# Features of q and k laid head-inside in each block of 128, and the transfers into the stack merged to one per slot and group of four heads

## The chip, the cores and the metric

One core of one Trainium2 chip. The metric is the device time of one execution in microseconds (us); the whole program is one launch.

## The reference, cut to what matters

Two cross-attention layers run one after the other over a batch of 16, with 256 query rows, width D = 512, 16 heads of 32 features. Layer 0 has a fused key/value projection over the 512 rows of context and query together, biases, an RMS norm and an MLP of hidden width 2048; layer 1 has a layer norm on the context, 256 keys and a gate. All in float32.

```
# layer 0 (b, 256 queries, 512 keys)
q  = (latents @ q_w + q_b).reshape(b, k_len, 16, 32)
kv = (concat(x, latents) @ kv_w + kv_b).reshape(b, p + k_len, 16, 32, 2)
attn = softmax(where(mask, einsum('bkhd,bnhd->bhkn', q, k) / 32, -inf))
a = einsum('bhkn,bnhd->bkhd', attn, v).reshape(b, k_len, 512) @ out_w + out_b + latents
out = gelu(rmsnorm(a) @ mlp_w1 + mlp_b1) @ mlp_w2 + mlp_b2 + latents
# layer 1 (b, 256 queries, 256 keys)
a = layer_norm(audio_kv);  Q = h @ Wq.T;  K = a @ Wk.T;  V = a @ Wv.T
attn = softmax(where(mask, Q K^T * 32**-0.5, -inf))
out = h + tanh(gate) * ((attn V) @ Wo.T)
```

Which of the 512 features of q and k sits in which row of an intermediate tile is free, as long as q and k agree and each head meets its own 32 features.

## The kernel before

The program is three stages: attention layer 0 (`attention_layer` with layer = 0), the MLP (`mlp`), attention layer 1. Both attention layers run the same code, one batch element per iteration, software-pipelined: iteration (p, a) prepares the projections of element p while the attention of element a = p - 1 runs. There are 15 iterations of a layer in which both halves are at work; the instruction streams of TensorE, VectorE, ScalarE, GpSimd and SyncE are written out by hand, each in its own block, tied by semaphores.

Numbers keep three products of float32 split in a high and a low part. For q and k this goes through the stack: a tile `stack` of 99 rows by 16 heads by 768 (layer 0) or 512 (layer 1) columns. Rows 0 to 31 (slot 0) hold a head's 32 high features of q and k, slot 1 (rows 32 to 63) q high beside k low, slot 2 (rows 64 to 95) q low beside k high; row 96 is the mask, rows 97 and 98 the softmax shift in two parts. One matmul with 97 rows then gives a head's scores (line 934), and one with 99 rows gives them shifted and transposed (line 959). The projections leave q and k in `qk` (layer 0: in `room`) with 128 feature rows to a block, that is four heads of 32 rows under each other, for four blocks g = 0 to 3. A half is two blocks, or eight heads.

SyncE (SP) issues every transfer, in order. In `load_stacks` (lines 307 to 321) it issues for each half and each j = 0 to 3 four transfers (32 rows, the two heads 4g + j of the half): 16 of them on line 311, and one for the mask row on line 319. SP's iteration (lines 363 to 405) is, in order: residual rows (367), layer 0's normalised rows out (370), next tokens (304, 305), then for each half the wait for `shift_copied` (ScalarE's line 538), two transfers of 8 rows of `shiftT` into rows 97 and 98 of the stack (379) and `spread_inverse` (354 to 361): eight transfers, each one row of reciprocals of the row sums spread over 32 rows of `norm_room` (359). Then `load_stacks` of both halves behind the wait on line 401 (TensorE has issued the last line 959 matmuls that read that half), and layer 1's output (405).

TensorE waits for a half of the stack at its first score (line 931), for the shift rows of a half at line 952, VectorE for the reciprocals of a half at line 712 before `normalise` (713), and TensorE's `project` (979) of block g needs that block normalised. ScalarE may write `qk` of the next element once the stack has been loaded from it (lines 512 and 517). In layer 0 the normalised values feed `turn_shift` and v through `o_norm_done` as well.

Weights are split into a high part (ScalarE, line 488) and a low part (VectorE, line 626) once per layer; the per-feature vectors are loaded on line 339 with a count `VECTORS` that GpSimd waits for before its memset of the stack (lines 465 and 470).

## Time and profile before

| | us |
|---|---|
| median of three executions (2630.4 to 2631.77) | 2631.36 |
| the profiled execution, its own time | 2632.31 |
| its span, first to last instruction | 2630.5 |
| TensorE matmul busy (share of the span) | 2443.7 (93%) |
| ScalarE busy | 1472.5 (56%) |
| VectorE busy | 1170.5 (44%) |

The stages by the clock of the trace: layer 0 to about 1100 us, the MLP to about 1823 us, layer 1 from there to the end. A row of the profile gives the engine (PE is TensorE's matmul, PEld its weight load, DVE VectorE, ACT ScalarE, POOL GpSimd, SPq SyncE's issue of transfers), and l_ before a name stands for either layer's tile. Lines 64 to 66 are the helper `product`, used by all projections and the MLP.

### The profile page before, as it was taken

The numbers are of one execution on the slowest core, as the hardware profiler recorded it, in microseconds if no ns is written. First come the engines' busy times: TensorE is split into PE (matmuls) and PEld (weight loads), VectorE is DVE, ScalarE is ACT, GpSimd is POOL, SyncE is SP. The second block draws the span as 40 slices with busy tenths as digits, with TensorE's granted clock in tenths as the row PEclk, the third lists the DMA queues.
The fourth block names the chain that finished last, engine by engine and source line by source line (L and its number), as shares of the span: only waits on it lengthen the run. The fifth ranks groups of instructions, "written<-read, shape, count | busy, mean of one in ns | idle before, by whom it ended". The sixth has DMA issues, their size and how long they took to land. (4 is left out here: it accounts for less than half of the span.)

```text
span 2630.5 us, 43959 instructions
## 1 busy us (share of the span) xinstructions
PE 2443.7 (93%) x14528; PEld 1913.9 (73%) x14528; DVE 1170.5 (44%) x2222; ACT 1472.5 (56%) x3354; POOL 226.2 (9%) x252
## 2 busy tenths in 40 slices
PE   6999999999999999899999999998888888888887
PEld 5677777777777777478888888887767677676674
DVE  4455555555555555452212221122655455455553
ACT  3777777777777777552222222222556566566564
POOL 1000000000000000000000000001211112112110
PEclk8999999999999999799999999999999999999998
DMA  6555555555555555341101110121566665656655
GB/s 173 106 114 113 113 113 113 113 113 113 109 115 112 112 112 97 76 140 49 48 0 48 48 48 0 48 80 64 106 130 124 118 138 102 127 131 109 132 100 86
DMA packets 172764, 255.82 MB, mean 97 GB/s; under 512 B 33793, under 2 KB 84257, under 8 KB 172721
## 3 DMA queue, kind: packets, MB, share of 16 engines
q1 hardware_dynamic: 172720, 255.27, 45.3%
q8 instruction: 24, 0.39, 0.1%
q14 instruction: 20, 0.16, 0.0%
HBM read 86.28 MB, written 25.21 MB: 42 GB/s over the span
## 5 line engine op out<-in xcount | busy, mean ns | idle before, releaser
L531 ACT ACTIVATE l_score_ps<-l_score_ps,l_neg_max 128x512 f32<-128x512 f32 (+1 forms) x1024 | 566.6, 556 | 338.3 <-DVE l_neg_max L696 337.9
L696 DVE TENSOR_REDUCE l_neg_max<-l_score_ps 128x1 f32<-128x512 f32 (+1 forms) x768 | 494.6, 684 | 149.7 <-PE l_score_ps L934 149.3
L544 ACT ACTIVATE l_probs<-l_score_ps 128x1024 f32<-128x1024 f32 x384 | 385.0, 1020 | 104.5 <-PE l_score_ps L959 103.0
L934 PE MATMUL l_score_ps<-l_stack 97*128 97x512 f32 (+1 forms) x1024 | 326.9, 379 | 80.4 <-DMA l_stack<-mask_rows 53.2
L1220 ACT ACTIVATE mlp_hidden<-mlp_hidden_ps,mlp_b_col 128x512 f32<-128x512 f32 x128 | 88.3, 690 | 496.2 <-PE mlp_hidden_ps L66 496.0
L959 PEld LDWEIGHTS l_score_ps<-l_stack 99*128 99x128 f32 x1536 | 213.9, 194 | 156.5 <-issue 81.6
L1255 DVE TENSOR_TENSOR mlp_hidden_l<-mlp_hidden,mlp_hidden_h 128x512 fp32r<-128x512 f32 x128 | 93.7, 732 | 518.3 <-ACT mlp_hidden_h L1222 518.3
L959 PE MATMUL l_score_ps<-l_stack 99*128 99x256 f32 x1536 | 277.7, 308 | 40.7 <-ACT l_probs L544 25.4
L934 PEld LDWEIGHTS l_score_ps<-l_stack 97*128 97x128 f32 x1024 | 181.4, 202 | 126.3 <-ACT l_score_ps L531 63.3
L974 PE MATMUL l_o_ps<-l_probs,l_v 128*32 128x256 f32 x3072 | 244.5, 398 | 1.8
L713 DVE TENSOR_TENSOR l_o_norm<-l_o_ps,norm_room 128x256 f32<-128x256 f32 x128 | 54.4, 425 | 401.0 <-PE l_o_ps L974 318.1
L531 ACT ACTIVATION_READ_ACCUMULATOR l_score_ps<-l_score_ps,l_neg_max 128x1 f32 x1024 | 211.6, 207 | 0.0
L64 PE MATMUL mlp_hidden_ps<-mlp_norm_h,mlp_w_l 128*128 128x512 f32 x512 | 200.3, 391 | 6.4 <-DVE mlp_norm_l L1250 6.4
L65 PE MATMUL mlp_hidden_ps<-mlp_norm_l,mlp_w_h 128*128 128x512 f32 x512 | 200.0, 391 | 0.0
L66 PE MATMUL mlp_hidden_ps<-mlp_norm_h,mlp_w_h 128*128 128x512 f32 x512 | 199.9, 390 | 0.0
L64 PE MATMUL mlp_sum_ps<-mlp_w_h,mlp_hidden_l 128*128 128x512 f32 x512 | 199.2, 389 | 0.0
L65 PE MATMUL mlp_sum_ps<-mlp_w_l,mlp_hidden_h 128*128 128x512 f32 x512 | 199.2, 389 | 0.0
L66 PE MATMUL mlp_sum_ps<-mlp_w_h,mlp_hidden_h 128*128 128x512 f32 x512 | 199.2, 389 | 0.0
L64 PE MATMUL l_item_ps<-l_hT_h,l_wk_l 128*128 128x512 f32 (+1 forms) x512 | 180.7, 353 | 11.0 <-DVE l_wk_l L626 5.8
L65 PE MATMUL l_item_ps<-l_hT_l,l_wk_h 128*128 128x512 f32 (+1 forms) x512 | 178.9, 349 | 0.0
L66 PE MATMUL l_item_ps<-l_hT_h,l_wk_h 128*128 128x512 f32 (+1 forms) x512 | 177.8, 347 | 0.0
L64 PE MATMUL l_item_ps<-l_hT_h,l_wq_l 128*128 128x256 f32 x512 | 150.4, 294 | 0.6 <-issue 0.6
(128 smaller groups left out, 4195.8 us busy)
## 6 DMA issues: line engine op xcount, KB each, us to landing
l_stack<-room SPq DMA_DIRECT2D x256, 192.0 KB
l_stack<-l_qk SPq DMA_DIRECT2D x256, 128.0 KB
l_stack<-room SPq DMA_DIRECT2D x128, 128.0 KB
norm_room<-l_shiftT SPq DMA_DIRECT2D x512, 32.0 KB, 4.0
l_stack<-l_qk SPq DMA_DIRECT2D x256, 64.0 KB
l_tokens<-in_x SPq DMA_DIRECT2D x16, 512.0 KB, 4.1
l_tokens<-in_ctx SPq DMA_DIRECT2D x16, 512.0 KB, 5.0
l_stack<-room SPq DMA_DIRECT2D x128, 64.0 KB
```

The costliest lines, as they stand in the source:

```text
L64: pe.matmul(out, left_l, right_h, start=start, stop=False)
L65: pe.matmul(out, left_h, right_l, start=False, stop=False)
L66: return pe.matmul(out, left_h, right_h, start=False, stop=stop)
L531: m = act.activation(e, e, ACT.Exp, bias=neg_max[:, q, h:h + 1], accum_out=row_sum[:, q, h:h + 1])
L544: act.activation(probs[:, s % PROBS, :].rearrange("p (a b) -> p a b", a=2), score_ps[:, 2 * (s % 2):2 * (s % 2) + 2, :], ACT.Exp).then_inc ...
L696: dve.tensor_reduce(out, bank, AXIS_X, ALU.max, negate=True).then_inc(max_done, 1)
L713: dve.tensor_tensor(o_norm[:, g % 2, :], o_ps[g % 2][:, 0:S], inv_sum[:, g, :], ALU.mult).then_inc(o_norm_done, 1)
L934: m = pe.matmul(out, stack[0:ROWS_MAX, h, P * q:P * (q + 1)], stack[0:ROWS_MAX, h, K_COLS], start=True, stop=True)
L959: n = pe.matmul(score_ps[:, 2 * (s % 2) + j // 2, S * (j % 2):S * (j % 2 + 1)], stack[0:ROWS_ALL, h, S + P * kb:S + P * (kb + 1)], stack[0 ...
L974: n = pe.matmul(o_ps[g % 2][to, 0:S], v[:, kb, DH * h:DH * (h + 1)], probs[:, s % PROBS, S * j:S * (j + 1)], start=(kb == 0), stop=(kb == ...
L1220: act.activation(hidden[:, m % HBUF, :], hidden_ps[m % 4][:, :], ACT.Gelu_apprx_tanh, bias=b1_col[:, m:m + 1])
L1255: dve.tensor_tensor(hidden_p[1][:, m % HBUF, :], hidden[:, m % HBUF, :], f32(hidden_p[0][:, m % HBUF, :]), ALU.subtract).then_inc(hidden_l ...
```

## The change

In every block of 128 features of q and k the order becomes (feature, head) instead of (head, feature): row 4d + j holds feature d of head j of the block. It is made where the weights are split: the source is read through `by_head` and the parts are written through `by_dim`, for wq and wk alone; their low parts take four instructions of VectorE in place of one. In layer 0 the biases of q and k are loaded block by block in the same order (12 vector transfers in place of 5). One transfer then takes 128 rows of `qk` of a block and writes 32 rows by four neighbouring heads of the stack: per block four transfers in layer 0, three in layer 1 (where the two of slot 0 become one), in place of eight per block before. The loads wait block by block. The two transfers of shift rows of a half become one, and the eight of reciprocals two, each with four source rows spread over 128 rows.

```diff
-    STACK_DMAS = HG * 4 + 1
+    GROUP_DMAS = 4 if first else 3
+    STACK_DMAS = GROUP_DMAS * GROUPS + 1
...
+        def by_dim(w):
+            return w.rearrange("p f (g d j) -> p (f g) j d", d=DH, j=HG)
+        def by_head(w):
+            return w.rearrange("p f (g j d) -> p (f g) j d", d=DH, j=HG)
...
-                    split_ops.append((c, kv[:, :, :, which], [t[:, 2 * c:2 * c + 2, :] for t in w], 1.0))
-            for u, w, scale in ((3, wq, SCALE), (2, wo, 1.0)):
-                src = stage[u % 2].rearrange("p (f n) -> p f n", f=FB)
-                split_ops.append((u, src, [t[:, :, :] for t in w], scale))
+                    src, parts = kv[:, :, :, which], [t[:, 2 * c:2 * c + 2, :] for t in w]
+                    if w is wk:
+                        src, parts = by_head(src), [by_dim(t) for t in parts]
+                    split_ops.append((c, src, parts, 1.0))
+            staged = [stage[u % 2].rearrange("p (f n) -> p f n", f=FB) for u in range(4)]
+            split_ops.append((3, by_head(staged[3]), [by_dim(t[:, :, :]) for t in wq], SCALE))
+            split_ops.append((2, staged[2], [t[:, :, :] for t in wo], 1.0))
...
-                    split_ops.append((u, score_ps[:, n % RING, :], [t[:, f, :] for t in w], scale))
+                    src, parts = score_ps[:, n % RING:n % RING + 1, :], [t[:, f:f + 1, :] for t in w]
+                    if u < 2:
+                        src, parts = by_head(src), [by_dim(t) for t in parts]
+                    split_ops.append((u, src, parts, scale))
...
-                return [(bq[:, :], column(vectors["q_b"])), (bk[:, :], kvb[:, :, 0]), (bv[:, :], kvb[:, :, 1]),
+                k_b = vectors["kv_b"].rearrange("(f j d two) -> f d j two", j=HG, d=DH, two=2)
+                q_b = vectors["q_b"].rearrange("(f j d) -> f d j", j=HG, d=DH)
+                return [*[(bq[:, f:f + 1], q_b[f]) for f in range(FB)],
+                        *[(bk[:, f:f + 1], k_b[f, :, :, 0]) for f in range(FB)], (bv[:, :], kvb[:, :, 1]),
                         (post_w[:, :], column(vectors["post_w"])),
                         (bo[:, :], vectors["out_b"].partition_broadcast(P))]
             return [(gamma[:, :], vectors["gamma"].partition_broadcast(P)), (beta[:, :], vectors["beta"].partition_broadcast(P)),
                     (gate[:, :], vectors["gate"].partition_broadcast(P))]
-        VECTORS = 5 if first else 3
+        VECTORS = 2 * FB + 3 if first else 3
         CONSTS = 3
-        INV_DMAS = HALF
+        INV_DMAS = GROUPS
 
         def load_tokens(sp, b):
             sp.dma_start(tokens[:, 0:QT, :], x_view[b]).then_inc(tokens_loaded, 16)
             sp.dma_start(tokens[:, QT:2 * QT, :], c_view[b]).then_inc(tokens_loaded, 16)
 
-        def load_stacks(sp, b, half):
-            def move(slot, j, to_cols, src):
-                heads = slice(HALF * half + j, HALF * (half + 1), HG)
+        def load_group(sp, g):
+            half, heads = g // GROUPS, slice(HG * g, HG * (g + 1))
+            def move(slot, to_cols, src):
                 sp.dma_start(f32(stack[DH * slot:DH * (slot + 1), heads, to_cols]), f32(src)
                              ).then_inc(stack_loaded[half], 16)
-            for j in range(HG):
-                src = qk[DH * j:DH * (j + 1), GROUPS * half:GROUPS * (half + 1), :]
-                move(0, j, Q_COLS, src[:, :, Q_HIGH])
-                move(0, j, K_COLS, src[:, :, K_HIGH])
-                move(1, j, slice(0, WIDTH), src[:, :, 0:WIDTH])
-                move(2, j, slice(0, WIDTH), src[:, :, WIDTH:2 * WIDTH])
+            if first:
+                move(0, Q_COLS, qk[:, g, Q_HIGH])
+                move(0, K_COLS, qk[:, g, K_HIGH])
+            else:
+                move(0, slice(0, WIDTH), qk[:, g, :].rearrange("p (n s) -> p n s", s=S)[:, 0:4:3, :])
+            move(1, slice(0, WIDTH), qk[:, g, 0:WIDTH])
+            move(2, slice(0, WIDTH), qk[:, g, WIDTH:2 * WIDTH])
+        def load_mask(sp, b, half):
...
-                for j in range(HALF):
-                    g, to = GROUPS * half + j // HG, slice(DH * (j % HG), DH * (j % HG + 1))
-                    sp.dma_start(inv_sum[to, g:g + 1, :],
-                                 shiftT[INV_ROW + j:INV_ROW + j + 1, half:half + 1, :].to_broadcast([1, DH, S])
+                for g in range(GROUPS * half, GROUPS * (half + 1)):
+                    row = INV_ROW + HG * (g % GROUPS)
+                    sp.dma_start(inv_sum[:, g, :], shiftT[row:row + HG, half:half + 1, :].to_broadcast([HG, DH, S])
...
-                        for part in range(2):
-                            sp.dma_start(
-                                f32(stack[SHIFT_ROW + part:SHIFT_ROW + part + 1,
-                                          HALF * half:HALF * (half + 1), Q_COLS]),
-                                shiftT[HALF * part:HALF * (part + 1), half:half + 1, :],
-                            ).then_inc(shift_loaded[half], 16)
+                        sp.dma_start(f32(stack[SHIFT_ROW:SHIFT_ROW + 2, HALF * half:HALF * (half + 1), Q_COLS]),
+                                     shiftT[0:2 * HALF, half:half + 1, :]).then_inc(shift_loaded[half], 16)
...
-                    for half in range(HALVES):
+                    for g in range(FB):
                         if a is None:
-                            sp.wait_ge(low_done, ITEMS * p + NT + NK + half + 1 if first
-                                       else ITEMS * p + NT + GROUPS * (half + 1))
+                            sp.wait_ge(low_done, ITEMS * p + (NT + NK + g // 2 + 1 if first else NT + g + 1))
                         else:
 
-                            sp.wait_ge(shifted_done, PSTEPS * a + PSTEPS // HALVES * (half + 1))
-                        load_stacks(sp, p, half)
+                            sp.wait_ge(shifted_done, PSTEPS * a + max(KB * (g + 1), 3))
+                        load_group(sp, g)
+                        if g % GROUPS == GROUPS - 1:
+                            load_mask(sp, p, g // GROUPS)
...
-                at_least(act, shift_loaded[half], 32 * a)
+                at_least(act, shift_loaded[half], 16 * a)
...
+                if len(src.shape) == 4:
+                    for j in range(HG):
+                        m = dve.scalar_tensor_tensor(low[:, :, j, :], src[:, :, j, :], scale, f32(high[:, :, j, :]),
+                                                     ALU.mult, ALU.subtract)
+                    m.then_inc(w_low, 1)
+                    return
...
-                u, ps, _parts, _scale = split_ops[n]
+                u, ps = split_ops[n][0], score_ps[:, n % RING, :]
...
-                    pe.wait_ge(shift_loaded[s // (2 * KB)], 32 * (a + 1))
+                    pe.wait_ge(shift_loaded[s // (2 * KB)], 16 * (a + 1))
```

## Rows read from the trace of the kernel before

**Rows 1.** The page: the chain that ended last, shares of the span by line.

```profile
SPq L311 10%; SPq L359 5%; ACT l_score_ps L531 2%; SPq L379 2%; DMA l_stack<-mask_rows 1%; DVE l_neg_max L696 1%; PE l_score_ps L934 1%; PE l_item_ps L64 1%; PE l_item_ps L65 1%; PE l_item_ps L66 1%; SPq L319 0%; ACT l_hT_h L508 0%; PE l_item_ps L870 0%; DMA l_stack<-l_shiftT 0%; ACT l_qk L513 0%
```

**Rows 2.** Waits in layer 1 (1890 to 2615 us): us in total, times, longest.

```profile
DVE l_o_norm L713 <- DMA norm_room<-l_shiftT: 82.9, 30, 7.5
...
PE l_score_ps L934 <- DMA l_stack<-mask_rows: 47.7, 23, 5.7
PEld l_score_ps L934 <- DMA l_stack<-mask_rows: 26.7, 13, 2.2
...
PE l_score_ps L959 <- DMA l_stack<-l_shiftT: 15.2, 15, 1.7
```

**Rows 3.** Layers 0 and 1: us, busy (count) by engine, granted clock, transfer share, GB/s.

```profile
90.00:1090.00 1000.00, 975.17 (x6288) 717.64 (x6286) 538.07 (x1051) 737.45 (x1539) 57.10 (x75) 0.99 0.56 110
...
1880.00:2600.00 720.00, 619.67 (x4359) 503.14 (x4358) 380.04 (x793) 445.11 (x1304) 92.39 (x112) 0.95 0.60 120
```

**Rows 4.** SP in one iteration of layer 1: start, duration, line, transfer, count.

```profile
2220.65 1.40 SPq L379 DMA_DIRECT2D l_stack<-l_shiftT  x2
...
2227.27 1.41 SPq L379 DMA_DIRECT2D l_stack<-l_shiftT  x2
...
2233.99 11.19 SPq L311 DMA_DIRECT2D l_stack<-l_qk  x16
...
2268.42 1.41 SPq L379 DMA_DIRECT2D l_stack<-l_shiftT  x2
```

**Rows 5.** PE and DVE in that iteration; in brackets idle time before, and releaser.

```profile
2199.78 0.74 PE L934 MATMUL l_score_ps<-l_stack 97*128 97x256 f32 x4 [1.80 <-DMA l_stack<-mask_rows]
...
2211.13 0.77 PE L934 MATMUL l_score_ps<-l_stack 97*128 97x256 f32 x2 [2.37 <-DMA l_stack<-mask_rows]
...
2231.09 0.73 PE L959 MATMUL l_score_ps<-l_stack 99*128 99x256 f32 x4 [1.01 <-DMA l_stack<-l_shiftT]
...
2237.93 0.42 DVE L713 TENSOR_TENSOR l_o_norm<-l_o_ps,norm_room 128x256 f32<-128x256 f32 x1 [2.89 <-DMA norm_room<-l_shiftT]
```

**Rows 6.** Stretches of that iteration, columns as in Rows 3.

```profile
2199.70:2204.30 4.60, 4.52 (x21) 4.20 (x22) 2.10 (x4) 2.91 (x10) 0.00 (x0) 0.63 0.63 147
...
2211.10:2214.40 3.30, 3.27 (x15) 3.30 (x16) 2.06 (x4) 2.21 (x11) 0.00 (x0) 0.51 0.42 142
```

**Rows 7.** Transfers moved at 2220.5 to 2222.5 us, then at 2213 to 2220.5 us.

```profile
DMA packets 16, 0.01 MB, mean 4 GB/s; under 512 B 8, under 2 KB 16, under 8 KB 16
...
DMA packets 816, 1.57 MB, mean 210 GB/s; under 512 B 48, under 2 KB 48, under 8 KB 816
```

**Rows 8.** Transfers moved at 2222.6 to 2230.6 us: GB/s in 40 slices, packets.

```profile
GB/s 31 10 0 10 36 36 26 21 36 36 21 36 26 26 31 26 26 31 26 26 31 21 36 26 62 62 154 128 31 20 31 36 21 26 36 20 72 92 62 41
DMA packets 447, 0.30 MB, mean 38 GB/s; under 512 B 151, under 2 KB 447, under 8 KB 447
```

**Rows 9.** Stretches of reciprocals, stack loads (layers 1, 0), tokens; columns as in Rows 3.

```profile
2227.20:2233.90 6.70, 5.35 (x49) 3.06 (x50) 2.87 (x5) 5.29 (x7) 5.50 (x6) 1.00 0.73 42
2246.00:2256.60 10.60, 8.86 (x50) 8.08 (x50) 5.60 (x9) 6.50 (x23) 0.00 (x0) 0.84 0.58 135
...
380.70:391.40 10.70, 10.68 (x52) 8.29 (x45) 6.17 (x11) 3.92 (x12) 0.00 (x0) 1.00 0.92 202
350.00:354.00 4.00, 3.94 (x28) 3.41 (x28) 3.03 (x6) 3.21 (x10) 0.00 (x0) 1.00 1.00 330
```

**Rows 10.** Timelines of SP and PE in one iteration of layer 0.

```profile
353.80 1.39 SPq L379 DMA_DIRECT2D l_stack<-l_shiftT  x2
...
367.03 0.74 PE L959 MATMUL l_score_ps<-l_stack 99*128 99x256 f32 x4
...
386.83 0.86 PE L934 MATMUL l_score_ps<-l_stack 97*128 97x512 f32 x3
```

**Rows 11.** Timeline of DVE at the start of layer 0.

```profile
17.95 8.59 DVE L616 TENSOR_SCALAR l_probs<-l_probs 16x256 f32<-16x256 int32 x1
```

**Rows 12.** Timeline of PE at the first scores of layer 1.

```profile
1867.69 0.47 PE L934 MATMUL l_score_ps<-l_stack 97*128 97x256 f32 x2 [1.80 <-DMA l_stack<-mask_rows]
```

## The prediction, made before the changed kernel was timed

> **What bounds the kernel now.** I read the chain of waits on the page first: after a fifth of the span the largest named parts of it are not arithmetic but SP issuing transfers, line 311 with 10%, 359 with 5%, 379 with 2% [rows 1]. Then the stretches by stage, to see where that chain counts. In layer 0 TensorE is busy 975 of 1000 us at a granted clock of 0.99; in layer 1 it is busy 620 of 720 us at 0.95 [rows 3]. So layer 0 is bound by TensorE, and the transfers can only cost something there; what the change can win lies in layer 1. The waits there say what ends the idle time: the mask row, which is the last transfer of a half of the stack (47.7 us on PE in 23 waits, others booked on PEld), and the shift rows (15.2 us in 15) [rows 2].
>
> One iteration of layer 1 takes 2268.42 - 2220.65 = 47.77 us [rows 4]. I count from T, the issue of the first shift rows (2220.65). Shift rows of half 1 have landed when PE goes on at T + 10.4; reciprocals of half 1 when VectorE goes on at T + 17.3; the first stack transfer is issued at T + 13.3; half 0 of the next element lets PE start its scores at 2199.78 + 47.77, that is T + 26.9, after 1.80 us of idling, so PE itself was ready at T + 25.1; half 1 is asked for 9.0 us later (2211.13 - 2.37 = 2208.76) and comes at 2211.13, a wait of 2.37 us [rows 4, 5]. Behind each of the two waits PE runs slowly: 4.6 us at a granted clock of 0.63 and 3.3 us at 0.51, mostly the lower level (1.2 GHz) instead of 2.4 GHz, which costs 4.6 x 0.37 + 3.3 x 0.49 = 3.3 us more [rows 6].
>
> **The change, part by part.** All times below are against the profiled execution (span 2630.5, own time 2632.3 us), which lies 0.95 us above the median; I take that off at the end.
>
> *Issue.* Per iteration of layer 1, line 311 goes from 32 transfers to 12, line 379 from 4 to 2, line 359 from 16 to 4. The 16 of a half take SP 11.19 us, so 0.70 each [rows 4]: 20 fewer are 14 us, the other 14 fewer some 9 us more. SP's work after T then ends before the data does: SP stops being the pace, and the question is how fast the data move.
>
> *How the transfers spread.* A transfer is over when each DMA engine that had a share has written its small completion packet. The transfer of eight shift rows shows 8 data and 8 small packets; three transfers over 128 rows (tokens and residual rows) show 48 small ones, 16 each [rows 7]. So the outermost count decides over how many engines a transfer is spread. The new stack transfers have 128 and 32 rows outermost: 16 engines. But the new reciprocals read 4 rows: I take it that they run on 4 engines, and the merged shift rows (2 rows written, 16 read) on 2. Everything behind them in those engines' order, the stack too, waits for them there. The Trainium skill ("DMA: Bandwidth & Descriptors", section "Why a DMA increments its semaphore by 16 and not by 1") gives just this rule, the largest number up to 16 that divides both outermost counts, and so 4 and 2; the trace agrees with it on 8 and 16 engines and has no case of 4 or 2.
>
> *Reciprocals.* Each half reads 8 rows, each 32 times: 256 packets of 1 KB, 262,144 bytes, now and after. Now they move at 38 GB/s on average, with a plateau near 27 GB/s and a burst above 100 [rows 8], while 16 engines are 73% busy at 42 GB/s, 3.6 GB/s per busy engine [rows 9]. So the source rows are the limit, not the engines. Bounds for four engines: at best each moves at the 20.6 GB/s of the token loads (330 / 16, rows 9), together 82 GB/s or 3.2 us per half; at worst each keeps its 3.6 GB/s, together 14.4 GB/s or 18.2 us; at the plateau rate 9.7 us. I take 38 GB/s, 6.9 us, since the source rows and the bytes are the same ones and four engines have three to four times the share each. Chain: T + 0.7 (one shift transfer) + 1.4 to the first packet (issued at 2220.65, and of the 2 us from 2220.5 only the last half us moves anything) [rows 4, 7] = T + 2.1; reciprocals of half 0 until T + 9.0; shift rows of half 1, 16 packets on 2 engines, 0.6 us, landed with 0.9 us at T + 10.5 (now 10.4); reciprocals of half 1 until T + 16.5, landed T + 17.4 (now 17.3). No gain and no loss there.
>
> *Stack.* A half of layer 1 is 8 heads x 96 rows x 2 KB = 1.57 MB. Now it moves at 135 GB/s with the engines 58% busy, starved by issue; in layer 0, with longer rows, the same kind of transfer shows 202 GB/s at 92% busy [rows 9]. I take 202: 7.8 us. The worst bound is that nothing gets faster (135 GB/s, 11.6 us), the best the token rate (330 GB/s, 4.8 us). The four slow engines start it at T + 16.5: half 0 is there at T + 16.5 + 7.8 + 0.9 = T + 25.2 against PE ready at T + 25.1, and half 1 at T + 33.0 against PE's need at T + 34.1. The waits of 1.80 and 2.37 us go, less 0.1: 4.1 us per iteration, x 15 = **-61 us** (the same as 30 waits of the mean 47.7 / 23 = 2.07 [rows 2]). The earlier, block-wise waits on `shifted_done` add to this margin and cost nothing: SP has nothing behind them but the same loads.
>
> *Clock.* Layer 1 lost 5% of 720 us, 36 us, to the lower level [rows 3]; the iteration above says 3.3 x 15 = 50. With both long waits gone most of it comes back, but the 1.0 us shift wait and the reciprocals' wait stay: **-25 us**, bounds 0 and -50. Scores that are not interrupted run closer to ScalarE and VectorE (445 and 380 us busy of 720, rows 3): I give back 0.5 us per iteration, **+8 us**.
>
> *First loads of layer 1.* PE waits 1.80 us for half 0 at 1867.69 [rows 12] and again for half 1, each with a slow clock behind: **-6 us**.
>
> *Layer 0.* Chain with 11.7 us per half (2.36 MB at 202 GB/s): half 0 at T + 16.5 + 11.7 + 0.9 = T + 29.1 with T = 353.8, need at 386.83, T + 33.0; shift rows of half 1 at T + 10.5, need at 367.03, T + 13.2 [rows 10]. Covered: 0. If the reciprocals take 9.7 us instead, half 0 comes at T + 34.7 and each of 15 iterations pays 1.7 us.
>
> *Setup.* Seven more vector loads on SP push back the mask and GpSimd's memset, and with them VectorE's 8.59 us of mask at 17.95 [rows 11], on which the key bias waits; two low parts in four pieces. **+5 us** (bounds 1 and 8); in layer 1, eight low parts of four pieces lie beside the layer norm: within that.
>
> Sum: -61 - 25 + 8 - 6 + 5 = -79 us; 2632.3 - 79 = 2553, against the median **2552 us**, 3.0% faster.
>
> **The rivals.** *The reciprocals fly.* Four engines on four different rows do not disturb each other: 3.2 us per half. Then the shift wait (15 us) and the whole clock loss (50 us) go too: -61 - 50 - 15 + 15 (ScalarE and VectorE set the pace) - 1 = -112, 2520 us; so too if they spread over all 16. For it speaks the burst above 100 GB/s in rows 8, against it the plateau.
>
> *The plateau holds.* 27 GB/s also for four engines. Shift rows land at T + 2.1 + 9.7 + 1.5 = T + 13.3, 2.9 us later than now; half 0 at T + 2.1 + 19.4 + 0.6 + 7.8 + 0.9 = T + 30.8, 3.9 later; half 1's wait and its clock (2.37 + 1.6) go. Layer 1 about 0 to -8, layer 0 +25, 2632 + 17 = 2649, less 1: 2648. The Trainium skill ("SBUF — State Buffer", section "Door 1: The DMA port swizzle") puts four neighbouring rows on one port, which speaks for this one.
>
> *Four engines are a bottleneck in themselves* (the slower end, one mechanism, its place lines 359 to 311). It decides at 26 GB/s: above about 10 us per half, half 0 comes so late that layer 1 has no gain left. At 14.4 GB/s, half 0 lands at T + 2.1 + 36.4 + 0.6 + 7.8 + 0.9 = T + 47.8, 20.9 us late, less 4.7: +16.2 x 15 = 243 us, and in layer 0 T + 51.7 against 33.0, +18.7 x 15 = 280: about 3150 us. Against it: 3.6 GB/s is what an engine gets when 16 share one row.
>
> *The stack does not move faster* than 135 GB/s: half 0 at T + 29.0, 2.1 late, half 1 still 2.6 us late; +2.3 x 15 = 35, 2666 us. Layer 0's 202 GB/s speaks against it.
>
> **How the numbers follow.** Forecast 0.57 (own range 2525 to 2590), reciprocals fly 0.20, plateau 0.12, four engines slower still 0.06, stack no faster 0.05. The range 2515 to 2645 us leaves out half of the last cases and the tails, some 0.18. A difference under 0.2% (5 us) could not be told from none; it needs a mixture near the plateau, 0.04; slower 0.18; faster 0.78.
>
> **What would show it.** In the profile after: SP issues 12 stack transfers per iteration of layer 1; PE's wait for the stack in layer 1 falls from 47.7 us to under 10; the packets of a reciprocal transfer come with 4 small ones; GB/s while they run is 38 (or 80, or 27); o_norm's wait for the reciprocals stays near 83 us; the clock of layer 1 rises from 0.95 to 0.98; layer 0's iteration stays at its length. Wrong if the shift rows of half 1 land past T + 12, or if a wait for the stack appears in layer 0.

## The result and the profile after

The changed kernel takes **2792.23 us** (median, 2786.19 to 2796.48) against 2631.57 for the kernel before: ratio 1.0605, 95% interval 1.0581 to 1.0629, **6% slower**. The forecast was 2552 us with a range to 2645. The profiled execution took 2791.4 us with a span of 2789.6.

The page of the changed kernel: the chain of waits by engine and by line.

```profile
DMA 12%; PE 12%; SPq 4%; issue 1%; ACT 1%; DVE 1%; DVEq 0%; POOL 0%; ACTq 0%; POOLq 0%
DMA l_stack<-mask_rows 8%; SPq L329 4%; DMA l_stack<-l_shiftT 4%; PE l_item_ps L64 2%; PE l_item_ps L66 2%; PE l_item_ps L65 2%; PE l_score_ps L955 2%; PE l_score_ps L980 1%; PE l_o_ps L995 1%; PE l_item_ps L891 1%; ACT l_score_ps L546 0%; PE l_o_ps L64 0%; SPq L340 0%; PE l_o_ps L65 0%; PE l_o_ps L66 0%
```

The change did what it says: issue mostly left the chain (line 329 has 4%, where line 311 had 10% and 359 had 5% [rows 1]). In its place stand the transfers themselves: `stack<-mask_rows` rose from 1% to 8%. The data are no longer asked for late; they arrive late. Where the 159 us of the two spans lie: the first stack transfer of layer 1 is issued at 1956.71 instead of 1853.79, so about 103 us are lost up to there, and from there to the end it is 832.9 instead of 776.7, 56 more in layer 1. The first shift rows of layer 0 are issued at 99.30 instead of 89.53, so some 10 of the 103 are lost before the iterations begin.

The waits for transfers in the changed kernel, first in layer 0 (150 to 1150 us), then in layer 1 (1980 to 2780 us): total, times, longest.

```profile
DVE l_o_norm L734 <- DMA norm_room<-l_shiftT: 88.2, 14, 6.3
PEld l_score_ps L955 <- DMA l_stack<-mask_rows: 54.8, 13, 4.3
PE l_score_ps L955 <- DMA l_stack<-mask_rows: 53.0, 14, 3.9
```
```profile
DVE l_o_norm L734 <- DMA norm_room<-l_shiftT: 65.1, 17, 8.3
PE l_score_ps L955 <- DMA l_stack<-mask_rows: 60.6, 27, 4.1
...
PE l_score_ps L980 <- DMA l_stack<-l_shiftT: 37.6, 16, 3.3
```

Of the two signs named as the end of the forecast one is there, a wait for the stack in layer 0. The other is not, though it came near: the shift rows of half 1 land at T + 11.5, not past T + 12. In layer 1 the waits for stack and shift rows grew instead of going [rows 2]. The stretches of the two layers say what it costs: in layer 1 the clock went from 0.95 to 0.88 and the transfer share rose while the GB/s fell [rows 3].

```profile
90.00:1150.00 1060.00, 979.77 (x6194) 721.29 (x6193) 521.89 (x1015) 715.81 (x1483) 53.23 (x70) 0.97 0.64 100
1980.00:2780.00 800.00, 674.16 (x4470) 534.77 (x4470) 383.25 (x807) 458.85 (x1346) 89.48 (x112) 0.88 0.65 110
```

One iteration of layer 1, SP's timeline (T = 2300.68), answers to [rows 4]; then PE's and VectorE's waits in it, which answer to [rows 5].

```profile
2300.68 0.73 SPq L398 DMA_DIRECT2D l_stack<-l_shiftT  x1
2301.45 1.22 SPq L380 DMA_DIRECT2D norm_room<-l_shiftT  x2
2305.40 1.13 SPq L398 DMA_DIRECT2D l_stack<-l_shiftT  x1
2306.57 4.88 SPq L380 DMA_DIRECT2D norm_room<-l_shiftT  x2
2311.57 9.10 SPq L329 DMA_DIRECT2D l_stack<-l_qk  x6
...
2321.76 4.05 SPq L329 DMA_DIRECT2D l_stack<-l_qk  x6
```
```profile
2312.16 0.73 PE L980 MATMUL l_score_ps<-l_stack 99*128 99x256 f32 x4 [2.32 <-DMA l_stack<-l_shiftT]
2332.26 0.74 PE L955 MATMUL l_score_ps<-l_stack 97*128 97x256 f32 x4 [2.28 <-DMA l_stack<-mask_rows]
2342.39 0.47 PE L955 MATMUL l_score_ps<-l_stack 97*128 97x256 f32 x2 [1.15 <-DMA l_stack<-mask_rows]
2312.39 0.42 DVE L734 TENSOR_TENSOR l_o_norm<-l_o_ps,norm_room 128x256 f32<-128x256 f32 x1 [3.26 <-DMA norm_room<-l_shiftT]
```

Two transfers that cost SP 1.22 us to issue take 4.88 the next time, and six that need 4.05 take 9.10: SP, which only issues, is held too. Shift rows come at T + 11.5 (forecast 10.5), half 0 of the stack at T + 31.6 (forecast 25.2, before 26.9), half 1 at T + 41.7 (forecast 33.0). The same iteration by stretches: reciprocals (2302.7 to 2316), then the stack.

```profile
2302.70:2305.40 2.70, 2.70 (x25) 2.69 (x24) 1.49 (x6) 2.44 (x10) 0.00 (x0) 1.00 0.20 26
2305.40:2312.00 6.60, 2.79 (x27) 1.42 (x25) 2.73 (x9) 3.83 (x4) 4.11 (x7) 1.00 0.22 37
2312.00:2316.00 4.00, 3.83 (x25) 2.24 (x26) 1.96 (x3) 2.35 (x3) 2.27 (x2) 0.66 0.25 58
...
2320.00:2324.00 4.00, 4.00 (x38) 2.16 (x34) 0.85 (x2) 1.87 (x3) 0.00 (x0) 0.98 1.11 132
2324.00:2328.00 4.00, 4.00 (x20) 3.04 (x17) 1.36 (x3) 0.42 (x1) 0.00 (x0) 1.00 1.07 130
2328.00:2332.00 4.00, 1.98 (x9) 1.31 (x7) 0.90 (x2) 0.00 (x0) 0.00 (x0) 1.00 1.12 131
2332.00:2336.00 4.00, 3.74 (x20) 3.46 (x21) 1.31 (x3) 2.47 (x10) 0.00 (x0) 0.72 1.10 129
```

The last two columns tell the case. While reciprocals run, the share is 0.20 to 0.25, that is three to four of 16 engines. While the stack runs the share is a little over 1 (I take the excess for overlapping packets), so all 16 are busy, and they still move only 129 to 132 GB/s, where the forecast had 202 at a share of 0.92 [rows 9]. Full engines at a low rate is not starvation by issue; each packet takes long.

### The profile page after: what moved, and what is told of

Its sections match the earlier page's. It is cut to its first block and busy times, and to the rows that moved or that the text cites. A ratio compares the mean times of both kernels' runs of the same rounds, so it can differ in the third digit from the quotient of the medians.

```text
span 2789.6 us, 43012 instructions
## 1 busy us (share of the span) xinstructions
PE 2511.5 (90%) x14528; PEld 1952.7 (70%) x14528; DVE 1175.1 (42%) x2255; ACT 1478.5 (53%) x3354; POOL 222.9 (8%) x252
## 5 line engine op out<-in xcount | busy, mean ns | idle before, releaser
L955 PE MATMUL l_score_ps<-l_stack 97*128 97x512 f32 (+1 forms) x1024 | 339.5, 392 | 143.3 <-DMA l_stack<-mask_rows 130.8
L980 PEld LDWEIGHTS l_score_ps<-l_stack 99*128 99x128 f32 x1536 | 222.0, 201 | 197.9 <-issue 121.6
L980 PE MATMUL l_score_ps<-l_stack 99*128 99x256 f32 x1536 | 286.5, 315 | 77.9 <-DMA l_stack<-l_shiftT 37.6
L995 PE MATMUL l_o_ps<-l_probs,l_v 128*32 128x256 f32 x3072 | 253.7, 411 | 1.8
```

What stands on the lines that cost most here:

```text
L955: m = pe.matmul(out, stack[0:ROWS_MAX, h, P * q:P * (q + 1)], stack[0:ROWS_MAX, h, K_COLS], start=True, stop=True)
L980: n = pe.matmul(score_ps[:, 2 * (s % 2) + j // 2, S * (j % 2):S * (j % 2 + 1)], stack[0:ROWS_ALL, h, S + P * kb:S + P * (kb + 1)], stack[0 ...
L995: n = pe.matmul(o_ps[g % 2][to, 0:S], v[:, kb, DH * h:DH * (h + 1)], probs[:, s % PROBS, S * j:S * (j + 1)], start=(kb == 0), stop=(kb == ...
```

## Experiments

Each version was timed beside the kernel before on the same chip (its medians there 2633.7 to 2635.2). The table sets medians of several chips beside each other, so differences of some 2 us in it mean nothing. "Neighbours" and "apart" are the source rows of a merged reciprocal transfer; each cell is the median in us:

| stack transfers | eight reciprocals | merged, neighbours | merged, rows apart |
|---|---|---|---|
| 32 rows, two shift transfers (before) | 2633.7 | 2735.3 | 2582.7 |
| 32 rows, shift merged | 2623.1 | | 2580.3 |
| 128 rows, two shift transfers | 2635.4 | | |
| 128 rows, shift merged (after) | 2605.6 | 2792.2 | 2628.3 |
| the same, stack rows interleaved | 2584.5 | 2632.5 | 2575.7 |

**1. Reciprocals back to eight transfers**, in the changed kernel.

```diff
-                for g in range(GROUPS * half, GROUPS * (half + 1)):
-                    sp.dma_start(inv_sum[:, g, :], shiftT[row:row + HG, ...].to_broadcast([HG, DH, S]))
+                for j in range(HALF):
+                    sp.dma_start(inv_sum[to, g:g + 1, :], shiftT[INV_ROW + j:INV_ROW + j + 1, ...].to_broadcast([1, DH, S]))
```

> The changed kernel with the eight reciprocal transfers per half of before in place of the two. Theory S (the loss is in the stack transfers: 16 engines are busy throughout and move only 128 GB/s, because four of them write into the same small group of stack rows at a time): little comes back, 2770 us, between 2740 and 2800, and the stack still moves at 120 to 135 GB/s. Theory R (the loss is that the merged reciprocals run on four engines and hold up the shift rows and the stack behind them): nearly all of it comes back, 2640 us or less.

2605.61 us (2602.19 to 2610.43), ratio 0.9895 (0.9879 to 0.9912). This one merge costs 187 us of the changed kernel.

**2. Only that merge, in the kernel before** (the reverse edit).

> The kernel before with only the reciprocals merged (two transfers per half of four source rows each). Theory S: close to before, 2615 to 2660 us, because these transfers are bound by the source rows either way and SP is relieved of 12 issues per iteration. Theory R: most of the loss appears, 2720 us or more, with the wait for the shift rows and for the reciprocals both grown.

2735.27 us, ratio 1.0383 (1.0365 to 1.0401): 101 us, with the transfers of the stack as they were. In layer 1 (1900 to 2550 us) PE's wait for the shift rows is 42.0 us, VectorE's for reciprocals 82.1, and SP, needing 10.26 us for 16 stack transfers when nothing is in front, needs 17.70 behind the reciprocals:

```profile
DVE l_o_norm L712 <- DMA norm_room<-l_shiftT: 82.1, 20, 4.9
PE l_score_ps L958 <- DMA l_stack<-l_shiftT: 42.0, 12, 4.6
```
```profile
2336.34 5.25 SPq L378 DMA_DIRECT2D l_stack<-l_shiftT  x2
2341.63 1.22 SPq L359 DMA_DIRECT2D norm_room<-l_shiftT  x2
2342.98 17.70 SPq L311 DMA_DIRECT2D l_stack<-l_qk  x16
...
2361.75 10.26 SPq L311 DMA_DIRECT2D l_stack<-l_qk  x16
```

**3. Stack rows interleaved by slot**, in the changed kernel: row 3d + slot in place of 32 slot + d, with the same transfers, sizes and counts.

```diff
-                sp.dma_start(f32(stack[DH * slot:DH * (slot + 1), heads, to_cols]), f32(src)
+                sp.dma_start(f32(stack[slot:MASK_ROW:SPLIT, heads, to_cols]), f32(src)
```

> The changed kernel with the stack's rows interleaved: feature d of slot s in row 3d + s instead of 32s + d. The same transfers, bytes and packets, but the engines that work at the same time write rows three apart. Theory S: the stack moves at 200 GB/s or more, its wait falls under 20 us in both layers, 2560 to 2630 us. Theory R: no change, 2780 to 2800 us.

2632.52 us, ratio 0.999 (0.998 to 1.0): the rows alone cost 160 us of the changed kernel. Its waits for the stack are gone, but with neighbours as source rows the granted clock of layer 1 falls to 0.90 (0.95 before); with rows apart (experiment 10, second line) it is 0.95:

```profile
1900.00:2500.00 600.00, 541.24 (x3656) 423.97 (x3657) 313.48 (x657) 365.06 (x1064) 80.11 (x99) 0.90 0.53 124
```
```profile
1900.00:2500.00 600.00, 560.03 (x3917) 441.65 (x3916) 338.72 (x731) 392.31 (x1144) 86.19 (x105) 0.95 0.52 132
```

**4. Both.**

> Both: interleaved stack rows and the eight reciprocal transfers per half of before. Theory S: 2540 to 2600 us, 0 to 30 us under the interleaved rows alone. Theory R: the same as with the eight reciprocal transfers alone. If both matter, it is faster than either by what each gives alone.

2584.51 us (2582.89 to 2590.22), ratio 0.9807 (0.9791 to 0.9824). The two edits, worth 187 and 160 alone, are worth 208 together: they overlap. One reason is in the stretches. First the version of experiment 1: its first stack load of layer 1, where no reciprocals run in front, and then its stack load behind reciprocals; under it experiment 3 at its first load and behind reciprocals.

```profile
1867.00:1871.00 4.00, 3.68 (x33) 3.44 (x31) 2.88 (x8) 2.03 (x5) 2.88 (x4) 1.00 1.13 130
1871.00:1875.00 4.00, 3.90 (x24) 3.10 (x25) 4.00 (x7) 2.92 (x6) 2.85 (x3) 1.00 1.07 128
...
2371.00:2375.00 4.00, 4.00 (x30) 2.73 (x21) 0.85 (x2) 0.42 (x1) 0.00 (x0) 1.00 1.10 185
2375.00:2379.00 4.00, 4.00 (x27) 3.57 (x26) 2.59 (x4) 0.45 (x2) 0.00 (x0) 1.00 1.09 181
```
```profile
1859.00:1863.00 4.00, 4.00 (x36) 4.00 (x35) 2.95 (x9) 0.93 (x2) 1.18 (x4) 1.00 1.10 233
1863.00:1867.00 4.00, 3.58 (x33) 3.37 (x31) 2.88 (x7) 2.50 (x5) 2.81 (x4) 1.00 1.08 214
...
2340.00:2344.00 4.00, 4.00 (x29) 2.42 (x28) 1.28 (x3) 0.53 (x2) 0.00 (x0) 1.00 1.09 210
```

A merged load into contiguous rows moves at 128 to 130 GB/s by itself. Behind eight 16-engine reciprocal transfers the same load moves at 181 to 185; behind merged ones it stays at 130. So experiment 1 did not only make room in front of the stack, it made the stack itself faster. Interleaved, it is 210 to 233 in all three stretches. That the reciprocals push the engines out of step, so that they no longer write neighbouring rows at once, would explain the 185; no run shows it.

**5. Reciprocals merged, source rows four apart**, in the changed kernel. `shiftT` gets 32 rows; the reciprocals of head j of block g lie in row 16 + 4j + g (each pair written twice, so that no row is left unset).

```diff
-                    sp.dma_start(inv_sum[:, g, :], shiftT[row:row + HG, half:half + 1, :].to_broadcast(...))
+                    sp.dma_start(inv_sum[:, g, :], shiftT[INV_ROW + g % GROUPS:SHIFT_ROWS:4, half:half + 1, :].to_broadcast(...))
```

> The changed kernel, but the four rows of reciprocals that one transfer spreads lie four rows apart in shiftT (rows 16, 20, 24, 28 and 17, 21, 25, 29) instead of next to each other (16 to 19, 20 to 23). Same two transfers per half, same bytes, same four engines. In the changed kernel a 1 KB packet of them takes 133 ns and the four engines together move 25 to 29 GB/s. If four neighbouring source rows share one way out of the memory (theory P), rows apart free it: a half goes from 9 us to 3.2 to 5 us, the stack starts 10 us earlier and moves at 180 GB/s and over, and the time falls to 2590 to 2640 us, about 2610. If it is what four engines can do with broadcast rows (theory E), nothing changes: 2785 to 2800 us. VectorE has one more reciprocal of 0.1 us or so per half, under 3 us in all.

2628.3 us (2619.66 to 2636.17), ratio 0.9971 (0.996 to 0.9983): 164 us back with the same two transfers, four engines and bytes. Theory P holds: the same four engines, bytes and counts of transfers, only other source rows. 2610 was 18 too low, because the expectation let the stack speed up with it, and it did not. Layer 1 keeps its stack wait and the load its rate; first the reciprocals of one half, then a stack stretch:

```profile
2332.00:2333.50 1.50, 1.50 (x15) 1.35 (x14) 0.93 (x6) 1.26 (x5) 0.00 (x0) 1.00 0.27 96
```
```profile
2305.00:2309.00 4.00, 0.96 (x5) 0.46 (x3) 0.00 (x0) 0.00 (x0) 0.00 (x0) 0.86 1.10 128
```
```profile
PE l_score_ps L958 <- DMA l_stack<-mask_rows: 57.7, 25, 3.5
```

Four engines move 96 GB/s from rows apart, 26 from neighbours, at about the same share of busy engines (0.27 and 0.20).

**6. Two rows per reciprocal transfer** (four transfers per half, two engines each), neighbours.

```diff
+                    for two in range(2):
+                        sp.dma_start(inv_sum[2 * DH * two:2 * DH * (two + 1), g, :], shiftT[row + 2 * two:row + 2 * two + 2, ...])
```

> The changed kernel, but with four transfers of reciprocals per half, each with two source rows (64 rows written), so that by the smaller outermost count two engines carry each. Theory E (each engine gets only so much from broadcast rows, 7.7 GB/s by the 133 ns of a packet): two engines move 15 GB/s, 17 us per half, the two halves end some 16 us later than in the changed kernel; both layers pay about that in each of their 15 iterations: 3200 to 3300 us. Theory P (the port of the neighbouring rows gives 25 to 29 GB/s however many engines pull): the packets get shorter (about 70 ns), a half stays at 9 to 10 us, and the time at 2790 to 2860 us.

2888.29 us, ratio 1.0966 (1.0948 to 1.0985): far from theory E's 3200, 28 over theory P's top. The rate decides for P: half the engines, the same 25 GB/s, now at a share of 10.9% where four engines had 0.20, so a packet took about half as long. The four transfers hold SP for 5.4 and 7.2 us per half, which P had not counted. The transfers moved at 2368 to 2372 us:

```profile
DMA packets 103, 0.10 MB, mean 25 GB/s; under 512 B 4, under 2 KB 103, under 8 KB 103
...
q1 hardware_dynamic: 103, 0.10, 10.9%
```

**7. The stack merge alone** (eight reciprocals, two shift transfers).

```diff
-                        sp.dma_start(f32(stack[SHIFT_ROW:SHIFT_ROW + 2, ...]), shiftT[0:2 * HALF, ...])
+                        for part in range(2):
+                            sp.dma_start(f32(stack[SHIFT_ROW + part:SHIFT_ROW + part + 1, ...]), shiftT[HALF * part:HALF * (part + 1), ...])
```

> Only the stack part of the change: eight transfers of reciprocals and two of shift rows per half, as before the change. Against the version with merged shift rows and eight transfers of reciprocals (2605.6 us) it shows the shift merge alone. If the merge to two engines matters little (16 packets): 2600 to 2612 us, SP issues 1.4 us more per iteration. If two engines held up the reciprocals behind them as four held up the stack: 5 to 15 us faster, 2590 to 2600.

2635.38 us (2630.35 to 2647.24), ratio 1.001 (0.9995 to 1.0024). Outside both expectations. The part of which the forecast hoped most, 20 fewer issues per iteration of layer 1, is worth nothing here; the shift merge is worth 30 us beside it (experiment 1). Over the 15 iterations of a layer, layer 1's shrink from 47.5 to 46.1 us in the mean, some 21 us in all; layer 0's grow from 65.7 to 66.5, some 13, and the first shift rows go out at 101.81 us instead of 89.53, another 12. What layer 1 wins is lost in layer 0 and at its start.

**8. The shift merge alone, in the kernel before.**

> The kernel before with one edit: one transfer of shift rows per half (two engines by the smaller outermost count) instead of two (eight engines each). In the changed kernel with eight reciprocal transfers this edit was worth 30 us (2635.4 against 2605.6). If that is the 1.4 us less issue per iteration ahead of reciprocals and stack, it is worth the same here, 10 to 30 us: 2605 to 2622 us. If it came only from the slow merged stack beside it, nothing here: 2628 to 2638. If two engines hold up the reciprocals behind them: over 2640.

2623.08 us (2618.14 to 2633.93), ratio 0.9948 (0.9932 to 0.9965): some 11 to 14 us, near the low end of the first expectation. Its five executions spread over 16 us, and the profiled one (2633.93) is the slowest of them, so no trace shows where the gain lies. Beside the merged stack the merge was worth 30; that difference is not explained.

**9. Reciprocals merged with rows apart, alone, in the kernel before.**

> The kernel before with one edit: reciprocals in two transfers per half of four rows each, and these rows four apart (merged with neighbouring rows the same edit made it 100 us slower, 2735.3). Theory P (neighbouring rows share one way out, 25 to 29 GB/s; apart about 96 GB/s): a half is over in 3 us, SP has no stall, the stack is issued about 5 us earlier and both stack waits of layer 1 go: 2555 to 2600 us. Rival (transfers on four engines hold up the 32-row stack transfers behind them even when fast): 2620 to 2650 us.

2582.65 us (2573.84 to 2585.14), ratio 0.9809 (0.9793 to 0.9825). With neighbours the same edit cost 101 us, apart it wins 51. All 32 issues of the stack are still there, but the stack starts earlier: at T + 8.6 (2286.54 - 2277.92) in one iteration, where it was T + 13.3. In layer 1 (1900 to 2500 us) the one wait for a transfer that is left on PE and VectorE is 4.4 us on the stack; the kernel before has 36.1 on the stack and 60.7 on reciprocals in that stretch. Yet the granted clock is what it was [rows 3]:

```profile
PE l_score_ps L936 <- DMA l_stack<-mask_rows: 4.4, 4, 2.0
```
```profile
1900.00:2500.00 600.00, 558.33 (x3935) 443.19 (x3936) 343.41 (x741) 395.05 (x1163) 84.83 (x104) 0.95 0.48 132
```

**10. Rows apart and interleaved stack**, in the changed kernel.

> The changed kernel with the reciprocals' source rows four apart and with the stack's rows interleaved by slot (row 3d + slot instead of 32 slot + d). Candidate for the best. Under theory P the stack moves at 215 to 230 GB/s from T + 11: 2570 to 2590 us, at or a little under the 2584.5 us of interleaved rows with eight transfers of reciprocals, and no wait for the stack in either layer. Under theory E as with interleaved rows alone: 2625 to 2640 us.

2575.67 us (2571.45 to 2578.2), ratio 0.9777 (0.9757 to 0.9796), the lowest median of all, no wait for the stack in either layer. One iteration of layer 1 takes 43.97 us (2336.42 - 2292.45).

With this run the two causes can be priced apart. Mean iteration, from the first issue of shift rows in a layer to that of its last iteration, over 15:

| stack rows | source rows of reciprocals | layer 0, us | layer 1, us | median, us |
|---|---|---|---|---|
| contiguous (after) | neighbours | 72.14 | 51.06 | 2792.2 |
| contiguous | apart | 66.17 | 46.52 | 2628.3 |
| interleaved | neighbours | 66.12 | 47.25 | 2632.5 |
| interleaved | apart | 65.78 | 43.89 | 2575.7 |
| kernel before | | 65.67 | 47.54 | 2631.6 |

Each fault alone costs 53 or 57 us against the version with neither; together they cost 217. A late start of the stack does harm above all when the stack is slow too.

**11. The two small merges without the stack merge**, in the kernel before.

> The kernel before with both small merges and the stack as it was: shift rows in one transfer, reciprocals in two transfers per half with source rows four apart. Against 2575.7 us of the version that also has the merged, interleaved stack it shows what the stack merge adds when nothing else is in its way. b_inv_apart has no wait of any size left for the stack (4.4 us in layer 1), so the merges of shift rows and stack can save little more: 2572 to 2584 us, and the stack merge is worth 0 to 8 us.

2580.28 us (2572.66 to 2585.73), ratio 0.9782 (0.9757 to 0.9807). Not to be told from experiment 10 by ratio: with rows apart the stack merge is worth nothing measurable.

**12. Interleaved rows in the kernel before.**

> The kernel before with one edit: rows of the stack interleaved by slot (3d + slot), its transfers of 32 rows as they were. If contiguous rows are slow only in the 128-row transfers of the change (128 GB/s without reciprocals ahead, against 211 to 233 with interleaved rows), nothing happens: 2626 to 2640 us, layer 1 being held by issue at 135 to 160 GB/s. If contiguous rows are slow for any transfer, the stack of layer 1 lands earlier: 2600 to 2620 us.

2635.07 us, ratio 1.0002 (0.9992 to 1.0012). No effect on the time. Layer 1 cannot show one, since issue holds its rate there; but in layer 0, where the 32-row transfers keep the engines nearly full, the rate is not better either: 195 GB/s at a share of 0.91 against 202 at 0.92 [rows 9]. Contiguous rows are slow only for the merged transfers.

**13. Stack loads waiting per half** instead of per block, in the version of experiment 1.

```diff
-                            sp.wait_ge(shifted_done, PSTEPS * a + max(KB * (g + 1), 3))
+                            sp.wait_ge(shifted_done, PSTEPS * a + KB * GROUPS * (g // GROUPS + 1))
```

> The changed kernel with eight reciprocal transfers per half, and its stack loads waiting per half as before the change instead of per block. Against 2605.6 us with block-wise waits. SP reaches the stack late in layer 1 anyway (T + 12), so the block-wise wait should be worth little: 2603 to 2615 us. If it is what lets the slow stack transfers start early in layer 0, 15 iterations of 1 to 2 us: 2620 to 2635.

2610.65 us (2609.16 to 2613.33) against 2605.6, as in the first expectation. The block-wise waits are worth 5 us at most to be seen: the intervals of the two ratios overlap (0.9899 to 0.9932, and 0.9879 to 0.9912).

**14 and 15. Each merged stack transfer in two (64 source rows) and in four (by head, 32 source rows)**, in the version of experiment 1, rows of the stack contiguous.

```diff
+                for j in range(0, 2):
+                    sp.dma_start(f32(stack[lo:lo + DH // 2, heads, to_cols]), f32(src[P // 2 * j:P // 2 * (j + 1)]))
```
```diff
+                for j in range(HG):
+                    sp.dma_start(f32(stack[DH * slot:DH * (slot + 1), HG * g + j, to_cols]), f32(src[j:P:HG]))
```

> The changed kernel with eight reciprocal transfers, its stack transfers (contiguous rows) each split in two of 64 source rows, 16 rows of the stack. Read at the first loads of layer 1, where no reciprocals run ahead. If the slow rate comes from how many engines write into neighbouring stack rows at once (theory N), 16 engines now write 16 neighbouring rows: the rate stays at 128 GB/s or so at a transfer share of 1. If it came from the length of the 128-row transfer, it rises towards 200. Whole time 2605 to 2640 us.

> The same, each stack transfer split in four by head: 32 source rows, four apart, into 32 rows of the stack for one head. Theory N: each engine has two rows of 32, as before the change, so bytes per busy engine rise from 128 to about 200 GB/s per full share; issue (24 transfers per half in layer 1, some 17 us) then holds it at 90 to 100 GB/s with a share of 0.5. If contiguous rows are slow whatever the split: 90 to 100 GB/s at a share of 0.75 to 0.8. Whole time by issue, some 10 us per iteration of layer 1 more: 2700 to 2850 us.

2610.7 us and 2937.99 us. One stretch of a stack load with nothing in front, in two, then in four, then of the kernel before:

```profile
1880.00:1884.00 4.00, 4.00 (x24) 3.23 (x24) 3.41 (x6) 2.39 (x4) 2.19 (x2) 1.00 1.09 127
```
```profile
2007.00:2011.00 4.00, 4.00 (x25) 3.14 (x24) 3.82 (x7) 2.59 (x5) 2.52 (x2) 1.00 0.29 99
```
```profile
1860.00:1864.00 4.00, 3.74 (x23) 2.98 (x24) 4.00 (x8) 3.08 (x6) 3.01 (x3) 1.00 0.68 158
```

GB/s by share of busy engines: 127 / 1.09 = 117 for 64 source rows, as for 128 (128 / 1.07 = 120); 158 / 0.68 = 232 before; 99 / 0.29 = 341 in four. The 341 is not a rate that 16 full engines would reach: at a share of 0.29 they seldom work at the same time, and the 32 source rows lie four apart. The fair comparison is between full engines writing the same contiguous rows: 202 / 0.92 = 220 for 32 source rows in layer 0 [rows 9] against 117 to 120 for 64 and 128; the changed kernel's own load of layer 0 moves 129 GB/s at a share of 1.05 (411 to 415 us). So contiguity alone does not do it; it takes a transfer of 64 or 128 source rows with it. In four it is held by issue (24 transfers, 16 us per half) and so worst in total; I had put 2700 to 2850.

## Why the prediction was wrong

Two steps failed: the rate of the reciprocals with "no gain and no loss there", and "I take 202" for the stack. With both mended (experiment 10) the time is 2575.7 us, 24 over the forecast, and what is left is the clock term.

*What bounds the kernel.* Half right. The waits for transfers in layer 1 were what could be won: experiments 9 and 10 remove those for the stack and for reciprocals, all but 4.4 us, and win 51 and 59 us. The issues of line 311 were not what made it: experiment 9 keeps all of them, experiment 7 takes 20 of 32 away and wins nothing. What counted was how early the stack starts, and that hung on the reciprocals in front of it. In experiment 10 the iteration of layer 1 shrinks by 3.80, where the forecast summed 4.1 less the 0.5 given back, and 1.7 more for the clock.

*Issue.* Right in number: 12 stack transfers per iteration, 4.05 us for six. Missing: SP is held when its transfers queue up behind slow engines (4.88, 9.10).

*How the transfers spread.* Right. In the first moments of that iteration (2300.5 to 2302.8 us) the shift transfer shows two small packets, not eight, and the reciprocals run at a share of 0.20 to 0.25, four of 16:

```profile
DMA packets 21, 0.02 MB, mean 8 GB/s; under 512 B 2, under 2 KB 21, under 8 KB 21
```

Here the rule of the Trainium skill ("DMA: Bandwidth & Descriptors", section "Why a DMA increments its semaphore by 16 and not by 1") holds on 2 and 4 engines too.

*Reciprocals: the first step that failed.* "I take 38 GB/s, 6.9 us" and "No gain and no loss there". While reciprocals ran alone, four engines moved no more from neighbouring rows than the plateau, 25 to 26 GB/s. So VectorE got half 0 at T + 11.7 instead of 9.9 and PE the shift rows of half 1 at T + 11.5 instead of 10.5; only the end of both halves, at about T + 15.3 (forecast 16.5), was not later, since the rate rises to 58 later on. The price of this step shows where the stack is fast: 2632.5 us with neighbours (experiment 3) against 2575.7 with rows apart (experiment 10), 57 us, nearly all of it in layer 1, where PE waited 23 us for shift rows and ran at a granted clock of 0.90 instead of 0.95. In the kernel before it was 101 us (experiment 2). With the slow stack behind them, neighbours instead of rows apart cost 164 (experiment 5).

The rival "the plateau holds" had this mechanism right. Its setting, neighbours with a fast stack, was run as experiment 3: 2632.5 against its 2648. The parts agree less well than the sum: it had +25 us in layer 0 and 0 to -8 in layer 1, the mean iterations say +7 and -4. Its page, the Trainium skill's "SBUF — State Buffer", section "Door 1: The DMA port swizzle", puts four neighbouring rows on one port; experiments 5 and 6 agree: 25 GB/s from neighbours with two or four engines, 96 from rows four apart.

*Stack: the second step that failed.* "I take 202." It moved at 129 to 132 in the changed kernel, and the rows written alone account for 160 us (experiment 3). The row behind the 202 was a transfer of 32 rows, and the new ones have 128; I treated the transfer of before as the same kind because rows, bytes and packet sizes agreed. Under the rate of 130 a half of layer 1 needs 12.1 us instead of 7.8. In the forecast's own chain that puts half 0 at T + 29.5; it came another 2 us later still. From 2316 to 2332 about 2.1 MB moved by the rows above (137 GB/s in the first 4 us), more than the 1.57 MB of a half, so some engines were already in half 1 while the late ones finished half 0. The rival "stack no faster" had 135 GB/s but priced only layer 1: in layer 0 it would have given 2.36 MB / 135 = 17.5 us per half, half 0 at T + 34.9 against the need at T + 33.0. Measured, it came at 425.90 = T + 37.5 (T = 388.41), and the iteration grew by 5.95 us, 89 us over 15. In layer 1 two iterations mean 51.2 us, 3.4 more, 51 over 15. That is the work of both steps together: with either one mended, layer 0's iteration is back at 66.1 to 66.2 us (table in experiment 10).

A rule that could have warned of it stands in the Trainium skill ("DMA: Bandwidth & Descriptors", section "The descriptor swizzle"): in a transfer to 128 rows each engine writes groups of four neighbouring rows, engines 0 to 7 in rows 0 to 63 and 8 to 15 in the rest. It is given for 128 rows written; that it holds for 128 rows read into 32 rows of four heads is my assumption. Then four neighbouring source rows are one feature of four heads, and 16 engines write stack rows 0 to 7 and 16 to 23 at once, which are four ports by the port map of the Trainium skill's "SBUF — State Buffer", section "Door 1: The DMA port swizzle". At the 25 GB/s that one port gave for reading in experiment 6 that is 100 GB/s as an estimate, and 200 for 32-row transfers on eight ports. Measured: 128 and 202, so the order is right and the first size is not. Which engine writes which row no trace here shows.

*Clock.* Wrong. The forecast gave back 25 us; the changed kernel lost (0.88), and even with all stack waits gone the clock stays at 0.95 (experiments 9 and 10). The low stretches moved. In the kernel before they lie behind the two waits for the stack [rows 6]. In experiment 10 the scores run at full clock, 2.4 GHz (first line), and instead TensorE runs at 1.2 GHz for 6.80 us of the attention (third line), after a stretch in which it was busy for 4.83 of 6.40 us (second line) and which ended in a wait of 1.57 us for ScalarE's probabilities. At the same place of the kernel before it was busy for 5.86 of 6.40 us (last line), waited 0.68 us, and the clock stayed at 1.00. Over layer 1 (1900 to 2500 us) these waits of PE for ScalarE grew from 8.2 to 20.4 us. So with the stack there in time TensorE meets ScalarE's pace instead, for which the forecast gave back 0.5 us per iteration but no clock. That this wait is the cause of the low stretch is read from its place; no run takes it away.

```profile
2299.50:2332.00 32.50, 31.07 (x223) 25.38 (x220) 17.93 (x36) 20.45 (x68) 1.96 (x2) 1.00 0.56 141
2332.00:2338.40 6.40, 4.83 (x41) 4.47 (x39) 4.75 (x16) 5.75 (x17) 0.67 (x3) 1.00 0.14 47
2340.50:2347.30 6.80, 6.80 (x36) 3.75 (x29) 2.10 (x4) 3.76 (x5) 4.84 (x4) 0.50 1.06 230
```
```profile
2338.35 0.73 PE L983 MATMUL l_score_ps<-l_stack 99*128 99x256 f32 x4 [1.57 <-ACT l_probs L559]
```
```profile
2221.00:2227.40 6.40, 5.86 (x50) 5.62 (x48) 4.61 (x15) 4.62 (x16) 0.73 (x3) 1.00 0.44 21
```

*Layer 0 free.* Wrong when both steps fail at once, as above: with one of them mended layer 0 pays 0.5 us per iteration, with neither 6.5. *Setup, +5.* Not seen, neither the vector loads nor the low parts: with interleaved rows the first shift transfer goes out at 88.85 us against 89.53 before; in the changed kernel it is 99.30, after 9.65 us of PE waiting for the first, slow stack load.

The rival "reciprocals fly" has its setting in experiment 10: 2575.7 against its 2520. Of the 56 us between them 50 are the clock gain it counted on, which never came; that these are the same 50 is a sum, not an experiment.

Still open: why a contiguous merged load speeds up to 185 GB/s behind 16-engine reciprocals, and why the shift merge is worth 30 us beside the merged stack and 11 to 14 without it.

## What to carry to other kernels

Merging transfers changes more than their number: it changes how many engines carry them, which source rows are read at once and which rows are written at once. Before merging, look at which source rows a broadcast reads together and which rows are written together; here one merge was worth -51 us with source rows four apart and +101 with neighbours. Take a rate for a new transfer only from one of the same number of rows, and look at GB/s together with the share of busy engines: here a share of 1 at a low rate went away when other rows were written, and a low share meant too few engines or late issue.

## What the runs showed of the hardware that was not expected

- Reading neighbouring rows gives 25 to 26 GB/s, with two engines or four; rows four apart give 96 with four.
- 16 busy engines moved 128 to 130 GB/s or 211 to 233 of the same data with nothing in front, by the rows written alone (experiments 1 and 3). 32-row transfers into the slow rows moved 202 at a share of 0.92.
- SP is held at its issues when slow transfers are in front: 16 issues took 17.70 us instead of 10.26.
- Taking away the waits behind which TensorE's clock fell did not raise the mean clock (0.95 before and after): it fell at another wait.
